# Rows of queries and keys gathered in the order feature, plane, for an attention layer on one core

## The reference, cut to what matters

```python
qkv = x @ Wqkv
q, k, v = split(qkv); 16 heads of 16
logits = einsum('bihd,bjhd->bhij', q, k) / 4 + SLOPES * (j - i), -inf where j > i
attn = softmax(logits); out = einsum('bhij,bjhd->bihd', attn, v) @ Wout
x = layernorm(x + out)
h = silu(x @ wg.T) * (x @ wu.T)
x = layernorm(x + h @ wd.T)
```

## Time and profile before

| | us |
|---|---|
| median of 3 runs | 2133.14 (2132.03 to 2133.5) |
| the profiled execution | 2131.38 |
| its span, first to last instruction | 2129.7 |
| PE busy | 1978.5 (93%) |
| DVE busy | 1596.0 (75%) |
| ACT busy | 1223.2 (57%) |
| POOL busy | 928.4 (44%) |
| traffic of SP's queue | 224.24 MB, 48.4% of the 16 DMA engines' time |
| mean granted clock of PE | 0.982 |

### The profile page before, as it was taken

The page is one execution under the profiler, slowest core; times in us unless marked ns, Lnnn a source line. Parts: engine busy times, 40 slices in busy tenths (PEclk is TensorE's granted clock), DMA queues, the critical chain, the costliest instruction groups (busy, mean ns, idle before and its releaser), DMA issues.

```text
span 2129.7 us, 47898 instructions
## 1 busy us (share of the span) xinstructions
PE 1978.5 (93%) x19236; PEld 1547.2 (73%) x19236; DVE 1596.0 (75%) x2772; ACT 1223.2 (57%) x1999; POOL 928.4 (44%) x1924
## 2 busy tenths in 40 slices
PE   2789999999999999999999999999999999999987
PEld 2557777777777778778777777777777777877766
DVE  3567777787777787777787777778777778777755
ACT  0456656556655655655655665655665565565553
POOL 0123444444444443444454444444444444344454
PEclk6799999999999999999999999999999999999998
DMA  6655455455455455545445545545545544554500
GB/s 139 155 103 122 102 112 113 100 111 119 110 112 115 97 114 107 120 112 106 108 104 107 129 101 112 113 99 111 119 108 113 116 97 113 108 120 101 96 22 21
DMA packets 148877, 228.34 MB, mean 107 GB/s; under 512 B 13600, under 2 KB 64544, under 8 KB 148640
## 3 DMA queue, kind: packets, MB, share of 16 engines
q1 hardware_dynamic: 148016, 224.24, 48.4%
q10 hardware_dynamic: 640, 1.05, 0.3%
HBM read 139.25 MB, written 84.20 MB: 105 GB/s over the span
## 4 chain that ended last, share of the span: by engine, by line
PE 79%; DVE 11%; ACT 5%; DMA 2%; issue 1%; POOL 1%; SPq 1%; POOLq 0%; DVEq 0%
PE pair L519 71%; PE pair L522 8%; DVE row_max L835 7%; ACT probs L753 3%; DVE staged_lo L820 2%; ACT staged_hi L733 2%; DMA q_rows<-bounce 1%; DVE row_max L837 1%; SPq L495 0%; DMA bounce<-staged_lo 0%; DVE row_max L832 0%; DMA probs<-L_attn_Wqkv 0%; DMA q_rows<-max_lo 0%; DVE x1t_lo L820 0%; POOL h_lo L961 0%
## 5 line engine op out<-in xcount | busy, mean ns | idle before, releaser
L753 ACT ACTIVATE probs<-pair 128x1024 f32<-128x1024 f32 x640 | 626.6, 1027 | 126.6 <-PE pair L519 126.6
L954 POOL TENSOR_SCALAR_AFFINE_SELECT probs<-probs 128x256 f32<-128x256 f32 (+1 forms) x896 | 371.5, 440 | 443.0 <-ACT probs L753 442.0
L961 POOL TENSOR_TENSOR h_lo<-h_fulls,h_hi 128x256 fp32r<-128x256 f32 x384 | 283.1, 738 | 503.5 <-ACT h_hi L778 492.8
L837 DVE TENSOR_REDUCE row_max<-pair 128x8 f32<-128x1024 f32 x256 | 312.6, 1221 | 112.4 <-PE pair L519 112.4
L519 PE MATMUL pair<-k_rows,q_rows 52*128 52x512 f32 (+3 forms) x2048 | 296.9, 348 | 88.1 <-DMA q_rows<-bounce 28.0
L835 DVE TENSOR_REDUCE row_max<-pair 128x2 f32<-128x1024 f32 x256 | 312.0, 1219 | 74.4 <-PE pair L519 74.4
L519 PE MATMUL pair<-q_rows,k_rows 64*128 64x512 f32 (+3 forms) x2048 | 316.9, 365 | 18.2 <-ACT probs L753 16.6
L519 PE MATMUL pair<-probs,v_ones 128*32 128x512 f32 (+3 forms) x4096 | 317.1, 439 | 2.0 <-POOL probs L954 1.5
L519 PEld LDWEIGHTS pair<-k_rows,q_rows 52*128 52x128 f32 x2048 | 176.7, 188 | 152.6 <-DVE row_max L835 65.1
L519 PEld LDWEIGHTS pair<-q_rows,k_rows 64*128 64x128 f32 x2048 | 165.1, 186 | 135.5 <-ACT probs L753 91.7
L733 ACT ACTIVATE staged_hi<-pair 128x512 fp32r<-128x512 f32 x128 | 76.5, 599 | 267.9 <-PE pair L519 258.5
(11 more groups left out here) (91 smaller groups left out, 3630.9 us busy)
## 6 DMA issues: line engine op xcount, KB each, us to landing
bounce<-staged_hi SPq DMA_DIRECT2D x128, 256.0 KB
bounce<-staged_lo SPq DMA_DIRECT2D x128, 256.0 KB
q_rows<-bounce SPq DMA_DIRECT2D x128, 256.0 KB, 5.2
k_rows<-bounce SPq DMA_DIRECT2D x128, 256.0 KB, 6.5
x_sb<-L_attn_x SPq DMA_DIRECT2D x32, 512.0 KB, 10.3
k_rows<-bounce SPq DMA_DIRECT2D x128, 128.0 KB, 6.0
q_rows<-bounce SPq DMA_DIRECT2D x128, 128.0 KB, 7.0
x<-L_attn_x SPq DMA_DIRECT2D x32, 512.0 KB, 9.0
```

Of the source, the lines that this page charges most:

```text
L753: scalar.activation(probs[g][:, tile, :, :], pair[:, :, :], ACT.Exp, scale=scale).then_inc(s_exp, 1)
L837: vector.tensor_reduce(maxima[:, QB2_PARTS:QB0 + 1, :, p].rearrange("p b s -> p s b"), pair[:, :, :].rearrange("p s (b n) -> p s b n", n=P ...
L954: made = pool.affine_select(out=diagonal, in_=diagonal, compare_op=ALU.is_ge, fill=0.0, base=0, pattern=[[0, diagonal.shape[1]], [1, P]], ...
L961: pool.tensor_tensor(h_lo[:, m, :], h_full[(n_split_h[step] - 1) % H_BUFFERS][:, :], h_hi[:, m, :].bitcast(F32), ALU.subtract).then_inc(s_ ...
```

## The change

The weights of queries and keys are put in another order when they are split at the start (`split_w`), so that a projection comes out with its partitions in the order (half and feature, pair) instead of (pair, half, feature). The bounce is then a plain copy of 128 rows of 2 KB, and four rows next to each other in it, 8 KB, are one partition of `q_rows` or `k_rows`. In these a plane now takes every fourth partition: partition 4a is plane 0 of feature a, 4a + 1 plane 1, 4a + 2 plane 2, and 4a + 3 one of the fixed rows or a row of the maxima. So

- a gather is six transfers of 32 partitions with 8 KB pieces, three planes of queries and three of keys, and a seventh, small one that puts zeros in the row of the low maxima, which the first pass now multiplies too;
- the first pass multiplies 63 rows instead of 52;
- the maxima are stored with two transfers instead of four;
- the table of fixed rows is written out for every pair (1 MB instead of 304 KB), copied in two parts behind the load of `w_qkv`, and filled in by two transfers for each buffer instead of eight;
- the split of each unit's weights is two casts and two subtractions of half the size, with the reads in steps of 32 elements;
- apart from that, in the last window the first norm stands behind the last `split_h` instead of ahead of it.

```diff
@@ constants
-    rows = np.zeros((ALIBI_ROWS * HEADS + COARSE_ROWS + MAX_ROWS, 2, tokens), np.float32)
+    rows = np.zeros((2, 2, 2, EDGE_ROWS, UNIT_PAIRS, tokens), np.float32)
...
@@ Plan
-    def down(self, b, part):
+    def down(self, b, part, norms):
         self.add("split_h", b, part, 5)
+        for step in norms:
+            self.add(*step)
         self.take("down", b, part)
...
-            if last:
-                self.add("norm1", done, 0)
-                self.add("norm1", done, 2)
             if has_ffn:
                 self.gate_up(ffn, 1, range(5, 6))
...
-                self.down(ffn, 1)
+                self.down(ffn, 1, [("norm1", done, 0), ("norm1", done, 2)] if last else [])
@@ build
-        bounce = nc.dram_tensor("bounce", [2, 4, HEAD_DIM, UNIT_PAIRS, 2, tokens], F32, kind="Internal").ap()
+        bounce = nc.dram_tensor("bounce", [2, 4, P, tokens], F32, kind="Internal").ap()
...
-        edge_fills, gathers, stores = 8, 8, 4
+        edge_fills, gathers, stores = 2, 7, 2
@@ sync
-            sync.dma_start(edge_copy, edge_rows).then_inc(s_edge_copied, 16)
             sync.dma_start(raw_qkv, w_qkv.rearrange("(k p) n -> p k n", p=P)).then_inc(s_qkv_in, 16)
+            for z in range(2):
+                sync.dma_start(edge_copy[z], edge_rows[z]).then_inc(s_edge_copied[z], 16)
...
-                        sync.dma_start(bounce[z, n].rearrange("d p s t -> (p s) d t"), source[:, side, :].bitcast(F32)).then_inc(s_bounced[z], 16)
+                        sync.dma_start(bounce[z, n], source[:, side, :].bitcast(F32)).then_inc(s_bounced[z], 16)
...
-                    for s in range(2):
-                        for rows, r0, n0, n in ((q_rows[z], 0, 0, 2), (k_rows[z], 0, 2, 1), (k_rows[z], 1, 2, 2), (q_rows[z], 2, 0, 1)):
-                            r = s * HALF + r0 * HEAD_DIM
-                            sync.dma_start(rows[r:r + n * HEAD_DIM, :, :].bitcast(F32),
-                                           bounce[z, n0:n0 + n, :, :, s, :].rearrange("n d p t -> (n d) p t")).then_inc(s_gathered[z], 16)
+                    for rows, r, n in ((q_rows[z], 0, 0), (k_rows[z], 0, 2), (q_rows[z], 2, 0), (k_rows[z], 1, 2), (q_rows[z], 1, 1), (k_rows[z], 2, 3)):
+                        sync.dma_start(rows[r::4, :, :].bitcast(F32),
+                                       bounce[z, n].rearrange("(a p) t -> a p t", p=UNIT_PAIRS)).then_inc(s_gathered[z], 16)
+                    e.wait_ge(s_edge[z], 16 * edge_fills)
+                    sync.dma_start(q_rows[z][MAX_LO_ROW::HALF, :, :].bitcast(F32), edge_copy[z, 0, :, EDGE_ROWS - 2, :, :]).then_inc(s_gathered[z], 16)
...
-                    for r, source in enumerate((max_hi, max_lo)):
-                        for s in range(2):
-                            row = s * HALF + MAX_ROW + r
-                            sync.dma_start(q_rows[u % 2][row:row + 1, :, :].bitcast(F32),
-                                           source[s * UNIT_PAIRS:(s + 1) * UNIT_PAIRS, :].bitcast(F32)).then_inc(s_max_stored[u % 2], 16)
+                    for row, source in ((MAX_HI_ROW, max_hi), (MAX_LO_ROW, max_lo)):
+                        sync.dma_start(q_rows[u % 2][row::HALF, :, :].bitcast(F32), source[:, :].bitcast(F32)).then_inc(s_max_stored[u % 2], 16)
@@ scalar, fill_edges
-                        for s in range(2):
...
+                        scalar.dma_start(rows[3::4, :, :].bitcast(F32),
+                                         edge_copy[z, side].rearrange("s e p t -> (s e) p t")).then_inc(s_edge[z], 16)
@@ vector, split_w
+                        cuts = [side * dim + part * P for side in range(2)]
+                        raw = [raw_qkv[:, :, c:c + P].rearrange("p k (h a) -> p k a h", h=UNIT_PAIRS) for c in cuts]
+                        hi, lo = ([t[:, :, c:c + P].rearrange("p k (a h) -> p k a h", h=UNIT_PAIRS) for c in cuts] for t in (wqkv_hi, wqkv_lo))
```

More of the change, by code:

```diff
@@ L23 @@
 TILES = 5
[L25 to L28, removed]
+EDGE_ROWS = HALF // 4
+ALIBI_ROWS, COARSE_ROWS = 4, 10
+MAX_LO_ROW, MAX_HI_ROW = HALF - 5, HALF - 1
+PASS1_ROWS = MAX_HI_ROW
 MASKED = -1.5e38
@@ L58, in constants @@
     ones = np.ones(tokens, np.float32)
-    rows = np.zeros((ALIBI_ROWS * HEADS + COARSE_ROWS + MAX_ROWS, 2, tokens), np.float32)
+    rows = np.zeros((2, 2, 2, EDGE_ROWS, UNIT_PAIRS, tokens), np.float32)
     stretch = np.arange(tokens) // -(-tokens // COARSE_ROWS)
     for h in range(HEADS):
[L62 to L69, removed]
+        q, k = (rows[h // UNIT_HEADS, side, h % 2, :, h % UNIT_HEADS // 2] for side in range(2))
+        q[0], k[0] = slope_hi[h] * ones, position
+        q[1], k[1] = slope_lo[h] * ones, position
+        q[2], k[2] = position, -slope_hi[h] * ones
+        q[3], k[3] = position, -slope_lo[h] * ones
+        for s in range(COARSE_ROWS):
+            q[ALIBI_ROWS + s] = stretch == s
+            k[ALIBI_ROWS + s] = np.where(stretch > s, np.float32(COARSELY_MASKED), np.float32(0))
+        k[EDGE_ROWS - 2] = k[EDGE_ROWS - 1] = -ones
     identity = np.eye(P, dtype=np.float32)
@@ L237, in rest @@
             if has_ffn:
-                self.down(ffn, 0)
+                self.down(ffn, 0, [])
             self.project(w + 2, 1)
@@ L383, in pair_of @@
             return pairs[plan.banks[step][0] // 2]
-        s_const, s_edge_copied, s_edge = sem("s_const"), sem("s_edge_copied"), [sem(f"s_edge{i}") for i in range(2)]
+        s_const, s_edge_copied, s_edge = sem("s_const"), [sem(f"s_edge_copied{i}") for i in range(2)], [sem(f"s_edge{i}") for i in range(2)]
         s_qkv_in, s_out_in, s_ffn_in = sem("s_qkv_in"), sem("s_out_in"), sem("s_ffn_in")
@@ L918, in _ @@
                     part, = key
-                    if part < 3:
+                    if part < 2:
                         e.wait_ge(s_qkv_in, 16)
-                        raw, hi, lo = raw_qkv, wqkv_hi[:, :, :], wqkv_lo[:, :, :]
-                        if part < 2:
-                            raw, hi, lo = (t[:, :, 0:2 * dim].rearrange("p k (s u n) -> p u k s n", s=2, u=2)[:, part] for t in (raw, hi, lo))
-                        else:
-                            raw, hi, lo = (t[:, :, 2 * dim:3 * dim] for t in (raw, hi, lo))
+                        cuts = [side * dim + part * P for side in range(2)]
+                        raw = [raw_qkv[:, :, c:c + P].rearrange("p k (h a) -> p k a h", h=UNIT_PAIRS) for c in cuts]
+                        hi, lo = ([t[:, :, c:c + P].rearrange("p k (a h) -> p k a h", h=UNIT_PAIRS) for c in cuts] for t in (wqkv_hi, wqkv_lo))
+                    elif part == 2:
+                        raw, hi, lo = ([t[:, :, 2 * dim:3 * dim]] for t in (raw_qkv, wqkv_hi, wqkv_lo))
                     else:
                         e.wait_ge(s_out_in, 16)
-                        raw, hi, lo = raw_out, wout_hi[:, :, :], wout_lo[:, :, :]
-                    vector.tensor_copy(hi, raw).then_inc(s_split_w, 1)
-                    e.wait_ge(s_split_w, 2 * part + 1)
-                    vector.tensor_tensor(lo, raw, hi.bitcast(F32), ALU.subtract).then_inc(s_split_w, 1)
+                        raw, hi, lo = [raw_out], [wout_hi[:, :, :]], [wout_lo[:, :, :]]
+                    for n in range(len(raw)):
+                        vector.tensor_copy(hi[n], raw[n]).then_inc(s_split_w, 1)
+                    e.wait_ge(s_split_w, SPLIT_W[part] + len(raw))
+                    for n in range(len(raw)):
+                        vector.tensor_tensor(lo[n], raw[n], hi[n].bitcast(F32), ALU.subtract).then_inc(s_split_w, 1)
                 elif kind == "as_float":
```

20 lines of the change are left out of this document (6 added, 14 removed).

## The result

The changed kernel takes **2111.16 us** (median of 4 runs, 2109.37 to 2112.87) where the kernel before takes 2133.32 (4 runs, 2132.03 to 2134.43). The ratio is 0.9896, 95% interval 0.9879 to 0.9913: 22 us less. The profiled execution is one of 2110.15 us, with a span of 2108.4.

A forecast was written before the change was run, and what follows sets the result against it. PE's own work was taken to bound the kernel from 200 to 2000 us, transfers only its start. Gains of 15.9 (first pass), 0.5 (maxima) and 1.2 (end) sum to 17.6: 2113.8 us profiled, 2115.5 as median, range 2107 to 2124.

The forecast's parts named there:

- Weights, split, bounce issue: At the start: weights 0.77 us earlier, DVE's split 1.6 us for 1.12, net -0.25; bounce issued at 16.3 us.
- Bounce: First bounce at the start: all 16 DMA engines for half, 5.5 us, landing at 21.9 (bounds 20.9 to 24.9).
- The rule's 2.7 us: Working rule for transfers: time is 2.7 us for start and receipt plus bytes / rate, taken from the first loads.
- Gather: First gather at the start: at 405 GB/s, since a transfer again spans 128 partitions, 7.9 us, landing at 29.8.
- case B: Rival on the first gather: it runs at 217 GB/s, takes 12.4 us; whole kernel 2120.0 (2117 to 2124); 25%.
- First pass: Start of the first unit's pass: 15.9 us earlier (11.4 at 217 GB/s), the chain behind it moving as a block.
- case C: Rival on the fill: gain handed back there, as if the second gather stayed late; 2129, up to 2133; 10%.
- Maxima: First unit's stored maxima: two transfers for four save 0.5 us (0 to 0.8) once, nothing in the steady part.
- End: Last window: POOL's norm1 steps moved, PE's 5 us wait for h_lo goes, norm late instead; gain 1.2 (0.5 to 1.7).
- Clock: PE's granted clock: dips may change places as all moves; +-4 us, one dip of 3.8 us more or fewer.
- Case D: Rival on PE's clock: more gained than summed, two dips fewer, 7.6 us; 2108 (2105 to 2111); 10%.
- E: Rival on the first pass: 63 rows for 52 cost PE the whole run; slower, 2150 (2133 to 2150); 5%.

## Why the prediction was right, and where not

The time lies in the range and the sign was right, but 4.3 us below the forecast: the sum of 17.6 was 3.6 us lower than the profiled execution's gain of 21.2. In part that is luck. The terms of the sum came to 15.2, 2.4 less than forecast, and a term of 6.3 us that the sum had at nothing, the clock, brought the whole above it.

- **Weights, split, bounce issue.** In at 7.46, forecast 7.41; the split takes 1.81, forecast 1.6 and within its bounds. But the bounce is issued at 17.51 and not at 16.3. PE's twelve projections took 5.50 us for 4.48. Pairs of them take 1.05 us at first and 0.63 later, and the step lies at 15.9 us for 13.3 before (timeline of PE, before and then after):

```profile
12.48 1.05 PE L519 MATMUL pair<-xt_hi,wqkv_lo 128*128 128x512 f32 x2
13.34 0.81 PE L519 MATMUL pair<-xt_hi,wqkv_hi 128*128 128x512 f32 x2
13.98 0.63 PE L519 MATMUL pair<-xt_lo,wqkv_hi 128*128 128x512 f32 x2
```

```profile
15.00 1.05 PE L519 MATMUL pair<-xt_hi,wqkv_lo 128*128 128x512 f32 x2
15.86 0.81 PE L519 MATMUL pair<-xt_hi,wqkv_hi 128*128 128x512 f32 x2
16.50 0.63 PE L519 MATMUL pair<-xt_lo,wqkv_hi 128*128 128x512 f32 x2
```

  In the other profiles with the new split the twelve take 4.53 to 5.50 us with the same work for PE, so the change doesn't set it; what does is not shown. I had taken PE's time as fixed.
- **Bounce.** 4.12 us, forecast 5.5 (bounds 4.6 to 8.6, so it is below them). The rule's 2.7 us for start and receipt came from the chain at the very start, and is too much for it: at 405 GB/s its 1.05 MB leave 1.5.
- **Gather.** 9.36 us, forecast 7.9, and 12.4 in case B. The choice between the two was right: with neighbours the gather takes 11.9 to 12.0 us, near case B. But my reason, the partitions that a transfer spans, is shown for that last step of 2.6 us alone. The other 8.6 us gained on the old gather have no cause that a run shows. The size was off too: 350 GB/s and not 405 make 2.7 + 2.1 / 0.35 = 8.7. Without the fill and the zeros beside it and from two queues, 7.7 is the least that was reached. One sign failed: the steady gather was to move over 300 GB/s and moves 287 to 295, nearer to that than to case B's 210.
- **First pass** 14.7 us earlier, forecast 15.9: 1.2 lost at the projections, 1.4 won at the bounce, 1.4 lost at the gather. It moved as a block: the second pass starts at 54.66 for 69.30, forecast about 53, so case C did not come. The second gather is issued from 34.99.
- **Maxima.** 0.5 forecast, nothing found. The wait of 0.8 us for `max_lo` is gone, with four transfers too.
- **End.** 1.2 forecast (0.5 to 1.7), 0.8 by the runs and 0.5 in the profile, where a dip at 2033 to 2037 takes the rest. The sum had both `h_lo` done at 2092.8, though two of 0.74 us begun at 2092.07 end at 2093.55. The last three here run from 2070.10 to 2072.47, which is 2092.9 counted from the transposes of `attn`; that the forecast fits is luck, since POOL begins the first of the two before PE comes. The wait for `h_lo` went and the norm is late in its place, as said.
- **Clock.** The term that failed. I saw that dips may move and took +-4 us around zero, at 3.8 us each. A dip of 3.5 to 4 us costs 1.4 to 1.6 (0.39 us for each at low clock), less than a half; PE is not alone on the chain there, which would explain it but is not shown. The stretch of 64 matmuls from which I had 3.8 was low for 7 us (75 to 82), and was PE's alone. And the sign was not even: the kernel before had 16.7 us more of low clock between the 1st and 5th unit than the changed one, and 4.3 more than any other profile here. Case D had the mechanism at 10%: two dips fewer, 7.6 us. It was 16.7 us less of low clock and 6.3 us.
- **E** is refuted: 348 ns with 63 rows, and a steady part of equal length.

## What to carry to other kernels

How far a transfer's partitions spread counts: the first gather, with 32 rows into every fourth of 128 partitions, moves at 344 to 371 GB/s, and with 32 neighbours at 205 to 242, with pieces of 2 KB as of 8 KB. In a steady gather it is 287 to 295 for 223. Before a rate in a window is read, look at what was issued just before it. A transfer that no wait of the busiest engine names can still cost the steady part, when it holds a staging tile (0.33 us a batch with four engines). When a stretch before the steady state moves, look at the clock in it first, and at several executions, before it is put down to the edit.

## What I had not expected of the hardware

- Issuing a plain transfer of 128 rows takes SP 0.35 to 0.45 us; the old bounce's first took 0.71, and a gather's with its 32 rows of 8 KB takes 0.51 to 0.60.
- A cast and a subtraction that read with a step, half the size each, take 0.36 and 0.55 us; the old ones of full size took 0.43 and 0.69. Size alone would have given 0.22 and 0.35.
- At the start matmuls run at little more than half the pace (a pair every 0.85 us for 0.47), up to 2.5 us longer in one execution than in another with the same matmuls, while the column of the granted clock shows 1.00 for both.
